# Preparation of a fused attention and expert kernel rebuilt: split parts stored once and repeated on loading, row maxima led by six steps in place of seven

## What is computed

```python
q, k, v = x @ Wq, x @ Wk, x @ Wv                      # split in 16 heads of 8
attn = softmax(q k^T / sqrt(128)) + bias              # bias: from a table of relative places
out  = layernorm(attn @ v) * gamma + beta
x    = layernorm(x + out)
sim  = (x @ hasher_w^T) @ keys^T                      # 32 experts, best 4, softmax of them
x    = layernorm(x + scale * sum_k w_k * (silu(x @ down_k) @ up_k))
```

## Time and profile before

| what | us |
|---|---|
| median of three runs (312.96 to 313.03) | 312.98 |
| the profiled execution | 312.77 |
| its span, from the first to the last instruction | 311.0 |
| outside the span | 1.8 |
| preparation: to the first score product | 41.4 |
| rounds 0, 1, 2, 3 (about) | 48.9, 59.7, 62.6, 58.4 |
| tail | 40.0 |

### The profile page before, as it was taken

The page is one execution under the profiler, slowest core; times in us unless marked ns, Lnnn a source line. Parts: engine busy times, 40 slices in busy tenths (PEclk is TensorE's granted clock), DMA queues, the critical chain, the costliest instruction groups (busy, mean ns, idle before and its releaser), DMA issues.

```text
span 311.0 us, 9808 instructions
## 1 busy us (share of the span) xinstructions
PE 283.6 (91%) x4087; PEld 131.2 (42%) x4087; DVE 231.8 (75%) x516; ACT 199.1 (64%) x392; POOL 125.8 (40%) x209
## 2 busy tenths in 40 slices
PE   4878988999998989999999999999999999889991
PEld 2545232333333333343455543434555433284390
DVE  4547788988889969987798699977986952167673
ACT  2575276777676767789865667898665689902500
POOL 8393511101102751127556312297563033943133
PEclk9999999999999999999999999999999999999997
DMA  6475597359432303000403020006000000100002
GB/s 171 103 235 175 144 322 122 80 207 308 179 99 57 81 4 78 6 2 17 140 4 78 4 78 5 3 8 184 4 2 6 2 5 1 36 4 2 0 6 62
DMA packets 28265, 23.48 MB, mean 76 GB/s; under 512 B 6542, under 2 KB 26686, under 8 KB 28222
## 3 DMA queue, kind: packets, MB, share of 16 engines
q1 hardware_dynamic: 27950, 22.73, 25.9%
q10 hardware_dynamic: 272, 0.13, 0.1%
HBM read 12.18 MB, written 10.52 MB: 73 GB/s over the span
## 4 chain that ended last, share of the span: by engine, by line
PE 62%; DVE 15%; POOL 8%; ACT 7%; issue 4%; DMA 3%; SPq 1%; POOLq 0%; DVEq 0%
PE sm_ps L1139 13%; PE st_ps L1139 11%; PE ov_ps L1189 11%; DVE neg_max L838 9%; PE si_ps L1139 6%; PE mi_ps L1139 5%; ACT probs L713 3%; PE mi_ps L1195 2%; PE st_ps L1412 2%; POOL rstd L466 2%; PE sm_ps L1150 2%; DVE stats L877 2%; ACT w_rows L624 1%; DMA k_stack<-stack_dram 1%; PE si_ps L1213 1%
## 5 line engine op out<-in xcount | busy, mean ns | idle before, releaser
L838 DVE TENSOR_REDUCE neg_max<-sm_ps 128x1 f32<-128x512 f32 x256 | 166.0, 685 | 37.1 <-PE sm_ps L1139 30.9
L713 ACT ACTIVATE probs<-st_ps 128x512 f32<-128x512 f32 x256 | 138.3, 613 | 41.7 <-PE st_ps L1139 41.7
L1139 PE MATMUL sm_ps<-k_stack,q_stack 96*32 96x512 bf16 x928 | 91.6, 383 | 4.5 <-DVE neg_max L838 3.9
L1139 PE MATMUL st_ps<-q_stack,k_stack 128*32 128x512 bf16 x1024 | 89.0, 380 | 1.3 <-ACT bias_v L624 0.7
L1189 PE MATMUL ov_ps<-probs,v_cur 128*32 128x512 f32 x512 | 66.5, 592 | 0.0
L1139 PEld LDWEIGHTS sm_ps<-k_stack,q_stack 96*32 96x32 bf16 x928 | 24.7, 94 | 64.6 <-DVE neg_max L838 52.7
L480 POOL TENSOR_TENSOR hid<-hid,w_rows 128x512 f32<-128x512 f32 x26 | 32.9, 1281 | 36.1 <-ACT w_rows L624 36.0
L1139 PEld LDWEIGHTS st_ps<-q_stack,k_stack 128*32 128x32 bf16 x1024 | 27.5, 96 | 34.8 <-ACT probs L713 16.0
L901 DVE SCALAR_TENSOR_TENSOR hid<-tanh_sb,mi_ps 128x512 f32<-128x512 f32 x24 | 16.3, 680 | 12.0 <-ACT tanh_sb L750 12.0
L1139 PE MATMUL mi_ps<-x_t,down_sb 128*32 128x512 f32 x192 | 25.0, 592 | 0.0
L1139 PE MATMUL si_ps<-up_sb,hid 128*32 128x128 f32 x768 | 24.0, 272 | 0.0
(11 more groups left out here) (166 smaller groups left out, 297.3 us busy)
## 6 DMA issues: line engine op xcount, KB each, us to landing
stack_dram<-parts SPq DMA_DIRECT2D x18, 384.0 KB, 4.5
q_stack<-stack_dram SPq DMA_DIRECT2D x16, 288.0 KB
k_stack<-stack_dram SPq DMA_DIRECT2D x16, 288.0 KB
stack_dram<-parts SPq DMA_DIRECT2D x6, 288.0 KB, 4.4
x_sb<-L_attn_x SPq DMA_DIRECT2D x4, 256.0 KB, 3.9
out<-y_out SPq DMA_DIRECT2D x3, 256.0 KB, 2.3
stack_dram<-parts SPq DMA_DIRECT2D x6, 96.0 KB, 2.1
down_sb<-L_ffn_values_down SPq DMA_DIRECT2D x1, 512.0 KB, 9.0
```

Of the source, the lines that this page charges most:

```text
L713: nc.scalar.activation(probs[:, u % 2, j, :], st_ps[:, score_bank(u * J + j), :], ACT.Exp, scale=SCORE_SCALE).then_inc(probs_ready, 1)
L838: nc.vector.tensor_reduce(neg_max[:, g % 2, col:col + 1], sm_ps[:, c % 2, :], AX.X, ALU.max, negate=True).then_inc(max_ready, 1)
L1139: i = nc.tensor.matmul(dst[n * TILE:(n + 1) * TILE], weights[:, n * TILE:(n + 1) * TILE], moving, **flags)
```

## The change

1. **Parts stored once.** `parts_dram` takes the place of `stack_dram`. `write_parts` writes each part once, and the nine pairs arise in `load_slice`: its source has a dimension of step zero that repeats rows three times. A row is now 4 heads by 512 in one piece (4 KB) where it was four pieces of 1 KB. The bytes loaded are the same, the bytes written a third. For sequence 0 each part is written as soon as it exists.
2. **Preparation reordered.** All of x is loaded first; the three weight matrices come over ScalarE's queue. x is turned for all sequences early, into four different banks, with `hid` as its buffer; v is copied by VectorE in place of ScalarE; the tables go to `mi_ps` and `si_ps`; the bias products to other banks. The tables' loads stand behind the first writes on SP. q and k of the last sequence are made at the very end of the preparation, and their parts partly inside round 0 (two copies of ScalarE in step 0, two and `half_scale` in step 3, GpSimd's part behind its first split).
3. **LEAD 6.** EARLY is 20. Twelve of these early products use four narrow column tiles in place of one wide one, as the bias products beside them do. In each round a group's maxima end four positions later. `shift1`, `shift2` and `shift0` stay in steps 2, 6 and 14; `shift3` goes from step 9 to 10. The last round makes maxima in its step 9 too.

```diff
-    LEAD = 7
+    LEAD = 6
-        stack_dram = nc.dram_tensor("stack_dram", [B, 2, H, D * PARTS * PARTS, S], BF16, kind="Internal").ap()
+        parts_dram = nc.dram_tensor("parts_dram", [B, 2, PARTS * D, H, S], BF16, kind="Internal").ap()
-                9: (["shift3", "o0"], ["down2"]), 10: ([], ["down3"]), 11: (["wt"], ["down4"]), 12: (["w0"], ["down5", "w1"]),
+                9: (["o0"], ["down2"]), 10: (["shift3"], ["down3"]), 11: (["wt"], ["down4"]), 12: (["w0"], ["down5", "w1"]),
...
                 for a, stack in enumerate((q_stack, k_stack)):
-                    src = stack_dram[t, a, g * J:(g + 1) * J]
-                    sp.dma_start(stack[0:TERMS, g * J:(g + 1) * J, :], src.rearrange("h r s -> r h s")) \
-                      .then_inc(stack_loaded[g], 16)
+                    rows = [[H * S, PARTS * D], [0, PARTS]] if a == 0 else [[0, PARTS], [H * S, PARTS * D]]
+                    src = bass.AP(parts_dram.tensor, (t * 2 + a) * PARTS * D * H * S + g * J * S, rows + [[1, J * S]])
+                    sp.dma_start(stack[0:TERMS, g * J:(g + 1) * J, :], src).then_inc(stack_loaded[g], 16)
...
-                for a in range(2):
-
-                    sp.wait_ge(*((first_split, a + 1) if b == 0 else (low_made, split_count(b, a))))
-                    rows = stack_dram[b, a, heads].rearrange("h (d i j) s -> (h d) i j s", i=PARTS, j=PARTS)
-                    for n in range(PARTS):
-                        dst = rows[:, :, n, :] if a == 0 else rows[:, n, :, :]
-                        sp.dma_start(dst, parts[heads.start * D:heads.stop * D, b, a]).then_inc(written, 16)
+                for i in range(PARTS):
+                    for a in range(2):
+                        if b:
+                            sp.wait_ge(low_made, split_count(b, a))
+                        else:
+                            sp.wait_ge(*((high_made, a + 1), (first_mid, a + 1), (first_split, a + 1))[i])
+                        rows = parts_dram[b, a, :, heads].rearrange("(i d) h s -> i h d s" if a == 0 else
+                                                                   "(d i) h s -> i h d s", i=PARTS)
+                        sp.dma_start(rows[i], parts[heads.start * D:heads.stop * D, b, a, i]).then_inc(written, 16)
             write_parts(0, slice(0, J), first_written)
+            load_tables()
...
+                    if u == 0 and is0(t):
+                        last_parts(0)
+                    if u == 3 and is0(t):
+                        middle_parts(B - 1)
+                        act.wait_ge(rows_loaded, 32)
+                        copy(half_scale[:], scale_sb[:], 0.5).then_inc(table_copied, 1)
```

More of the change, by code:

```diff
@@ L548, in _ @@
             pool.wait_ge(spread_made, PARTS)
+            add_beta(3)
+            split_shift(0, 0)
+            for n, a in enumerate((1, 0)):
+                pool.wait_ge(last_copied, n + 1)
+                nc.gpsimd.tensor_sub(resid[:, 1, a], resid[:, 1, a], parts[:, B - 1, a, 0, :]).then_inc(last_resid, 1)
             def round_(t, attention, experts, more, late):
@@ new lines, in x_copy, with high_parts @@
+            def x_copy(b):
+                act.wait_ge(x_turned, b + 1)
+                copy(x_t(b), turned_bank(b)).then_inc(xt_copied, 1)
+            def high_parts(b):
+                for a in range(2):
+                    act.wait_ge(qk_made, 2 * b + a + 1)
+                    copy(parts[:, b, a, 0, :], qk_bank(b, a)).then_inc(high_made, 1)
+            for dst, src, loaded in ((wq_sb, w_q, proj_loaded[0]), (wk_sb, w_k, proj_loaded[1]), (wv_sb, w_v, proj_loaded[2])):
+                nc.scalar.dma_start(dst[:], src).then_inc(loaded, 16)
@@ new lines, in _ @@
+            pe.wait_ge(consts_made, 2)
+            turn_x(0)
+            turn_x(1)
+            pe.wait_ge(proj_loaded[0], 16)
+            make_qk(0, 0)
+            pe.wait_ge(proj_loaded[1], 16)
+            make_qk(0, 1)
+            turn_x(2)
+            turn_x(3)
+            pe.wait_ge(proj_loaded[2], 16)
+            make_v(0)
+            make_qk(1, 0)
+            make_qk(1, 1)
+            make_v(1)
+            make_qk(2, 0)
+            make_qk(2, 1)
+            make_v(2)
+            pe.wait_ge(high_made, 4)
@@ new lines, in _ @@
+            pe.wait_ge(resid_made, 4)
+            pe.wait_ge(rel_loaded, 16)
+            for n in range(NWIN // P):
+                i = turn(mi_ps[:, n * P:(n + 1) * P], rel_win[:, n, :], ident[:])
+            i.then_inc(table_mm, 1)
+            make_v(3)
+            pe.wait_ge(keys_loaded, 32)
+            turn(si_ps[0:PD, 0:NE], keys_sb[:], ident[0:NE, 0:NE]).then_inc(table_mm, 1)
+            pe.wait_ge(xt_copied, B)
+            early_maxima(2)
+            pe.wait_ge(table_copied, 2)
@@ L1360, in _ @@
+                    early_maxima(1, product=tiled)
+            early_maxima(EARLY, J * C + 2, tiled)
+            pe.wait_ge(table_copied, 3)
+            make_qk(B - 1, 1)
+            pe.wait_ge(consts_made, 8)
+            pe.wait_ge(shift_split, 1)
+            turn(mi_bf[:, 0:P], shift_parts[:].rearrange("p i n -> p (i n)"), ident_bf[:]).then_inc(misc_ready, 1)
+            early_maxima(1, EARLY)
+            bias_turn(CG)
+            early_maxima(2, EARLY)
             bias_turn(G - 1)
+            early_maxima(2, EARLY)
@@ L1384, in score @@
                                 scores(t, u, j)
-                    spread = not any(here(n, *kind) and n[:2] in ("do", "up") for n in jobs_at(kind, u - 1)[1])
+                    spread = not any(here(n, *kind) and n[:2] in ("do", "up") for n in jobs_at(kind, u - 1)[1]) \
+                        and not (is0(t) and u == 0)
                     score(*range(1 + spread))
                     maxima(0)
+                    if is0(t) and u == 0:
+                        pe.wait_ge(bias_copied, G - CG)
                     score(*range(1 + spread, 3))
```

256 lines of the change are left out of this document (120 added, 136 removed).

## The result

The changed kernel takes 319.08 us (median of four runs, 317.69 to 320.82), the kernel before 313.00 beside it: a ratio of 1.0196, 95% interval 1.0146 to 1.0247. It is slower by 2%, and above the range of the prediction, which ended at 316.8. Two of the twelve executions of one later version (`best1`, 315.44 and 315.67) fell in a slower state of the chip and are left out of its figures. The first view is the page of the kernel after, the parts that answer to the earlier trace rows: span, granted clock by slice, transfers, chain.

A forecast was written before the change was run, and what follows sets the result against it. TensorE (62% of the chain) and VectorE (15%) set the rounds, transfers the preparation. Terms -2.3 + 1.25 + 0.2 + 0.3 + 0.8 = +0.25 on 312.77 or 312.98 gave 313.0 or 313.2; forecast 313.3, 8-in-10 range 308.7 to 316.8 us.

The forecast's parts named there:

- shift 1, round 0: Step 2 of round 0: the group's last maximum comes four positions later, so the turn waits for its split; +1.25 us.
- other shifts; ScalarE: Rounds 0 to 3: six split ends near their turns, +0.2 in all; round 0: copies ahead of ScalarE's exponentials, +0.3 us.
- last round: Step 9 of the last round gains four maxima at 0.22 us of TensorE each (0.9 together); +0.8 us.
- shorter lead: Rival, turns behind the first: if each of 15 waited 0.25 us, 3.8 us more; chance 0.05.
- the prediction's doubt about source or target: New k load: three engines if a small outer count in the source limits width; twelve if the target alone counts.
- the sum up to the first scores: Preparation: first load, writes, loads of groups 1 to 3, then shift 0; first scores 39.1 for 41.40, -2.3 us.
- 30 x 0.165 = 5.0, with 1.0 for lead and landing: Preparation, first load: 30 rows on each of three engines; from issue at 14.3 to first maxima at 20.3 us.
- 2.2 us, plus 0.4: Preparation: the other writes behind the first load on the same engines, 6 x 8 pieces of 1 KB; until 22.9 us.
- only one write is left: Preparation, SP: at about 12.0 one write of about 0.59 us remains to issue, so the load could go at 14.1.
- a 4 KB row is dearer: Rival, preparation: each 0.01 us more a row costs 1.2 us; 316.2 at 0.19, 324 at 0.26; chance 0.11.
- The rival of twelve engines: Preparation: k load as wide as q's; first scores near 34.9, -6.5 us there, 309.4 in all; chance 0.29.
- The clock: Before round 0: TensorE idle some 3 us; if its granted clock fell there, it would cost some tenths.

The follow-up runs named there:

- best1: A later version whose change the text does not state under this name; two of its twelve executions, 315.44 and 315.67 us, are left out.
- the wide load: The changed kernel with each load of k's rows issued as three loads of 24 rows, on twelve DMA engines: 311.95 us, ratio 0.9957 to the kernel before.
- the front order: q and k of sequence 0 made ahead of the turn of the next x; added to the wide load with a lead of seven (310.42 us): 310.03 us.
- qk_first: Kernel with k's loads split onto twelve engines and a lead of seven, plus q and k of sequence 0 ahead of the next x's turn: 310.03 us, ratio 0.9886.

## Why the prediction was wrong

| step | predicted | measured |
|---|---|---|
| load of q issued | 14.3 | 14.87 |
| first maxima | 20.3 | 24.00 |
| loads of groups 1 to 3 begin | 22.9 | 25.95 |
| shift 0 lands | 39.1 | 44.25 |
| first scores | 39.1 | 44.30 |
| preparation | -2.3 | +2.9 |
| shift 1, round 0 | +1.25 | +1.3 |
| other shifts; ScalarE | +0.2; +0.3 | under 0.1 each |
| last round | +0.8 | +0.85 |

**Right: the mechanism and the rounds.** k on three engines, a lone shift load behind k's rows, the wait of 1.21 us at shift 1 (steps 2 and 3 together +1.27), the last round, rounds 1 and 2 unchanged. That shorter lead leaves the other turns alone was right too: +0.04 and -0.06 us in rounds 1 and 2. Round 0 ended at +0.95 and not +1.3, since steps 0, 1 and 9 to 11 gave back 0.4. The Trainium skill, page "DMA: Bandwidth & Descriptors", section "Rules for kernel authors", states the case itself: a leading broadcast of c copies with zero step confines the whole transfer to at most c engines. The trace agrees (3.1 engines for c = 3), and the prediction's doubt about source or target is settled: the small number in the source is enough.

**Wrong: the sum up to the first scores, by 5.2 us.** The failed term is the one of the first load and the remaining writes, "30 x 0.165 = 5.0, with 1.0 for lead and landing", then "2.2 us, plus 0.4". From q's issue to the first maxima it has 6.0 us, and 9.1 were measured. The first maxima are 3.7 us late, and 3.05 of that are left at 25.95; the second half, from there to the shift's landing, is off by another 2.1. Mis-sized were:

- *The issue.* q's load left at 14.87 in place of 14.3. x landed at 4.3 in place of 3.57, but the last low part was there at 12.11, as assumed. Wrong was "only one write is left": the write of k's middle part held SP until 12.0, so two were left, of some 0.6 us each. Then k stands behind q, and the issue of a load in the new form takes 0.71 to 0.84 us where the earlier trace rows has 0.31 for q. k left SP at 15.76, some 1.1 us after the time that the sum implied.
- *The neighbours.* 0.165 is the price with three engines alone. In the first load q's rows and the writes ran beside k's. The run with the writes held back puts 1.35 us down to the writes. I had seen the two prices, 0.165 and 0.26, and took the low one "since three engines alone resemble rows 8 most": true for groups 1 to 3 later, false for the first load, which ran in company.
- *The load itself.* With the writes held back it still takes 6.74 us from k's issue where the sum left 5.65: another 1.1, of which I have no closer account.
- *The queue behind.* At 23.54 k's last piece of the first load was through, with some 125 of the 576 pieces of the writes still to come, and SP waits for them before the next load; so most of the delay is passed on. From 25.95 on, 90 rows took from about 27.4 to 43.2 us, 0.176 each: 1.0 us for the rows, and the rest for the start, 1.45 us after the issue where I had 0.6, and for the landing of the shift.

The rival "a 4 KB row is dearer" was the nearest in size, but not the cause: alone the row cost 0.160. (Its far end, by its own terms, is 324.6 and not 324.) All these errors have the same sign, for the sum followed the shortest way through a stretch with one path and no cover; a range for that stretch should have leaned to one side.

**The rival of twelve engines** was off in the same way. It gave first scores near 34.9; with twelve engines they came at 39.09. Of these 4.2 us, 2.2 lie ahead of q's issue (1.23 of it the wait for the second x, where the prediction had at most 0.3 for turning it), 1.2 in the first load, whose four issues alone took 2.2, and 1.4 in the sixteen maxima, at a fallen clock; 0.6 came back behind them. Even that kernel, at 311.95, is 2.5 us above its forecast of 309.4.

**The clock.** I expected a fall before round 0 that would cost tenths. In the profiled execution it fell earlier, ahead of the first maxima, to 1.2 GHz. There it stretched the sixteen maxima to 11.84 us, where they take 10.32 with TensorE kept busy, but the scores waited for the shift's load behind k's rows all the same. It did not fall before round 0 after 3.33 us of idle time; in the run with TensorE kept busy it did, after 3.38, and cost 1.0 us in two steps. Under the wide load the cover is gone: idle for 2.66, 2.84 and 2.95 us ahead of the first maxima, TensorE fell to the lower clock in three traces, and in the three with 1.58 to 1.66 us it did not; there the sixteen maxima took 11.97 to 11.99 us and here 10.32. That is the larger part of what the front order shows in its trace.

**Still open** is the spread: the runs of the changed kernel span 3.1 us, those of its versions 1.4 to 4.5, and those of the kernel before 0.15 beside the changed one and up to 2.9 in the longer series beside the experiments. Two things on record go with it. The mean granted clock does: in the kernel before all spans of 310.8 to 311.9 us have 0.992 or more and all of 312.9 to 313.7 have 0.987 to 0.989; in `qk_first` three spans of 307.0 to 307.3 have 0.996 and two of 308.1 and 308.4 have 0.991. Whether the clock is the cause there or fell because something else kept TensorE waiting is not shown. And with the second x turned ahead of q, that load came late in two of eight traces (waits of 1.23 and 1.30 us): q's load then left at 16.5 and not at 14.87 to 15.55. In the three traces with q and k first it left at 15.28 to 15.65.

## What to carry over

A load that repeats rows by a dimension of step zero looks like a saving of bytes and issues, but it is as wide as that dimension: look at the outer count of both sides before anything else, and split it into several wide loads (7 us here for two more issues a group). A price read where a few engines work alone holds only there; where transfers run side by side take the crowded price, and follow the queue behind a narrow load to the small transfer that the next stage waits for. When a transfer is moved on one issuing engine, list everything behind it down to the next load that someone waits for. And ask of a fallen clock what it lies under: here it cost nothing ahead of the scores while a transfer was the bound, and 1.65 us once the transfer was out of the way.

## What the runs showed of the hardware

- A piece of 4 KB took 0.160 us with three engines at work and 0.30 with twelve; the rate went from 79 to 165 GB/s for four times the engines.
- A load of 12 KB took 5.87 us from issue to landing behind the rows of the same three engines, and 2.5 under the wide load, issued when k's last rows were all but through; with one group fewer ahead of it the first exponential came 2.4 us earlier.
- A load whose source repeats rows took SP 0.71 to 0.84 us to issue in the preparation, where the 72-row form took 0.31 to 0.43; three loads of 24 plain rows took 1.34 together.
- The experts' table took SP 6.49 us to issue while k's rows of two groups were still on their way, and 4.15 to 4.33 once they were through; the load of the shift behind it had to wait.
- Ahead of the first maxima TensorE's granted clock went to 0.50 after 2.66 to 2.95 us without work and stayed at 1.00 after 1.58 to 1.66; at 0.50 the sixteen maxima took 12.0 us in place of 10.3. Ahead of round 0 it stayed after 3.33 us in one trace and fell after 3.38 in another.
- In the first microseconds the fp32 product of q takes 2.05 us and later 1.02, though the records give a granted clock of 1.00 for both; ten turns ahead of it changed nothing.
